# Attention of the last two tiles ended by token halves, the halves' steps alternated, output units placed behind step 7

## What is computed

```python
Q = elu(x @ Wq.T + bq) + 1;  K = elu(x @ Wk.T + bk) + 1;  V = x @ Wv.T + bv
KV = einsum('bnd,bne->bde', K, V);  Z = einsum('bnd,bd->bn', Q, K.sum(axis=1) + 1e-06)
x = layernorm(x + (einsum('bnd,bde->bne', Q, KV) / Z[..., None]) @ Wo.T + bo)      # (8, 512, 128)
# the same rows seen as 8 steps of a gated recurrence for 512 tokens, c: (512, 128)
ft = sigmoid(xt @ wf.T + c @ uf.T + bf);  it = sigmoid(xt @ wi.T + c @ ui.T + bi)
gt = tanh(xt @ wc.T + c @ uc.T + bc);     c = ft * c + it * gt
h = tanh(x @ wo.T + c_final @ uo.T + bo);  x = layernorm(x + h)
```

## Time and profile before

| | before |
|---|---|
| median of the runs | 103.84 us (103.84 to 103.92, 3 runs) |
| profiled execution | 104.32 us |
| its span | 102.4 us |
| granted TensorE clock over the span | 0.983 |

### The profile page before, as it was taken

The page is one execution under the profiler, slowest core; times in us unless marked ns, Lnnn a source line. Parts: engine busy times, 40 slices in busy tenths (PEclk is TensorE's granted clock), DMA queues, the critical chain, the costliest instruction groups (busy, mean ns, idle before and its releaser), DMA issues.

```text
span 102.4 us, 1942 instructions
## 1 busy us (share of the span) xinstructions
PE 93.8 (92%) x615; PEld 80.7 (79%) x615; DVE 80.6 (79%) x235; ACT 67.5 (66%) x140; POOL 42.7 (42%) x65
## 2 busy tenths in 40 slices
PE   5998999999799999999999999999999999979610
PEld 4878788688388978878899899989899999768400
DVE  3226388989999997799589989996544999999870
ACT  1427579479387784966769445599365949779450
POOL 2006198417647238108405803360400056456870
PEclk9999999999999999999999999999999999999985
DMA  2867999000000000000000000000000000145336
GB/s 36 299 250 287 389 400 341 16 0 3 0 0 0 0 0 0 3 6 0 0 0 0 0 0 6 0 3 3 6 0 0 0 0 6 62 143 174 134 102 205
DMA packets 5414, 7.36 MB, mean 72 GB/s; under 512 B 508, under 2 KB 3229, under 8 KB 5405
## 3 DMA queue, kind: packets, MB, share of 16 engines
q1 hardware_dynamic: 4972, 6.92, 19.1%
q10 hardware_dynamic: 432, 0.33, 1.1%
HBM read 5.15 MB, written 2.10 MB: 71 GB/s over the span
## 4 chain that ended last, share of the span: by engine, by line
PE 57%; DVE 27%; issue 5%; ACT 4%; POOL 3%; DVEq 0%; POOLq 0%; ACTq 0%
PE ps_k L408 7%; PE ps_ctx L431 6%; PE ps_q L422 6%; PE ps_ctx L451 5%; DVE stats L1119 5%; PE ps_f L395 4%; DVE x L1108 4%; DVE x L939 3%; PE ps_x L465 2%; DVE s L990 2%; DVE x L954 2%; DVE new L983 2%; POOL rstd L331 2%; PE ps_ctx L441 2%; DVE x L1135 2%
## 5 line engine op out<-in xcount | busy, mean ns | idle before, releaser
L344 POOL TENSOR_TENSOR s_lo<-s,s_hi 128x512 fp32r<-128x512 f32 (+1 forms) x8 | 8.0, 1011 | 24.6 <-ACT s_hi L753 24.6
L331 POOL TENSOR_TENSOR rstd<-var_eps,minus_half 128x4 f32<-128x4 f32 (+1 forms) x9 | 9.2, 1022 | 12.9 <-DVE var_eps L1127 12.8
L315 POOL TENSOR_TENSOR rstd<-var_eps,minus_half 128x4 f32<-128x4 f32 x8 | 8.6, 1078 | 6.6 <-DVE var_eps L930 6.5
L306 POOL TENSOR_TENSOR k_pair<-k_rows 128x256 f32<-128x256 f32 x8 | 6.3, 782 | 9.8 <-DVE k_rows L965 9.8
L939 DVE TENSOR_SCALAR x<-x,stats,rstd 128x128 f32<-128x128 f32 x26 | 10.0, 441 | 0.0
L408 PE MATMUL ps_k<-wkq,x_cols 128*128 128x128 f32 x64 | 9.4, 294 | 0.0
L723 ACT ACTIVATE k_exp<-ps_k,minus_one 128x512 f32<-128x512 f32 x8 | 5.5, 686 | 5.5 <-PE ps_k L416 4.6
L408 PEld LDWEIGHTS ps_k<-wkq,x_cols 128*128 128x128 f32 x64 | 8.7, 209 | 0.3
L790 ACT ACTIVATE x_hi<-ps_x 128x512 fp32r<-128x512 f32 x8 | 4.8, 594 | 6.2 <-PE ps_x L465 6.2
L737 ACT ACTIVATE th_f<-ps_f,half_b 128x256 f32<-128x256 f32 (+1 forms) x11 | 5.8, 530 | 4.4 <-PE ps_f L511 4.2
L422 PE MATMUL ps_q<-x_cols,wkq 128*128 128x512 f32 x16 | 8.2, 597 | 0.0
(11 more groups left out here) (197 smaller groups left out, 291.5 us busy)
## 6 DMA issues: line engine op xcount, KB each, us to landing
x_cols<-xt SPq DMA_DIRECT2D x8, 256.0 KB, 7.3
x_rows<-x SPq DMA_DIRECT2D x8, 256.0 KB, 7.3
out<-x SPq DMA_DIRECT2D x7, 256.0 KB, 2.2
wgate<-w_gate SPq DMA_DIRECT2D x1, 384.0 KB, 6.4
out<-x SPq DMA_DIRECT2D x2, 128.0 KB, 2.0
wkq<-w_kq ACTq DMA_DIRECT2D x1, 131.0 KB, 3.4
wvo_in<-w_vo_in ACTq DMA_DIRECT2D x1, 128.0 KB, 3.3
wout<-w_out SPq DMA_DIRECT2D x1, 128.0 KB, 6.9
```

Of the source, the lines that this page charges most:

```text
L315: nc.gpsimd.tensor_tensor(rstd[:, b], var_eps[:, b], minus_half[:], ALU.pow).then_inc(rstd_ok, 1)
L331: nc.gpsimd.tensor_tensor(part_of(rstd, u, T), part_of(var_eps, u, T), minus_half[:, 0:nt * H].rearrange("p (t c) -> p t c", c=H), ALU.pow ...
L344: nc.gpsimd.tensor_tensor(s_lo[:, t % 2, part], state(t)[:, part], s_hi[:, t % 2, part].bitcast(F32), ALU.subtract).then_inc(slo_ok[k], 1)
```

## The change

The attention of tiles 6 and 7 no longer ends by whole tiles. HALVES lists four halves j: (6, first), (7, first), (6, second), (7, second). Each has its own statistics, variance, root, normalisation, turn, high copy and low part. Halves 0 and 1 are normalised by VectorE, 2 and 3 by ScalarE. They are turned into ps_x1, ps_ctx, ps_x1 and ps_q. The low part of the second halves of tiles 5, 6 and 7 is made by GpSimd from x1_cols instead of by VectorE from PSUM; the first halves' stays on VectorE.

Steps 8 and 9 change places: 8 is now (5, second), 9 is (7, first), so the first and the second half alternate from step 6 on. s_lo of step 8 comes from GpSimd, and that of step 10 is still VectorE's, but now ahead of second_residual(1).

On TensorE out_x(0) and out_x(1), which stood behind gates_s(6) and gates_s(7), now stand behind gates_s(9) and gates_s(10), and gates_x(10) ahead of out_s(0). On ScalarE state_high(10) stands ahead of out_tanh(1), normalise(0) ahead of out_tanh(2), and out_tanh(8) ahead of normalise(5). On VectorE second_normalise(0) stands ahead of second_residual(2). The number of DMAs and their order are unchanged.

```diff
 STEPS = [(0, 0, C), (1, 0, C), (2, 0, C), (3, 0, C), (4, 0, H), (5, 0, H), (4, H, C), (6, 0, H),
-         (7, 0, H), (5, H, C), (6, H, C), (7, H, C)]
+         (5, H, C), (7, 0, H), (6, H, C), (7, H, C)]
...
-SHARED_LN = (0, 6, 7)
+WHOLE = 6
+HALVES = [(6, 0), (7, 0), (6, H), (7, H)]
+SHARED_LN = (0,)
+ACT_HALVES = (2, 3)
...
+        turn_bank = [ps_x1, ps_ctx[:, 0], ps_x1, ps_q]
+        def half_cols(j):
+            return slice(HALVES[j][1] * D, (HALVES[j][1] + H) * D)
+        def turned_half(j):
+            return turn_bank[j][:, half_cols(j)]
...
+            def half_root(j):
+                b, c0 = HALVES[j]
+                pool.wait_ge(var_half_ok, j + 1)
+                nc.gpsimd.tensor_tensor(rstd[:, b, c0:c0 + H], var_eps[:, b, c0:c0 + H], minus_half[:, 0:H],
+                                        ALU.pow).then_inc(rstd_half_ok, 1)
+            def half_shift(j):
+                b, c0 = HALVES[j]
+                pool.wait_ge(minus_mean_half_ok, ACT_HALVES.index(j) + 1)
+                pool.wait_ge(rstd_half_ok, j + 1)
+                nc.gpsimd.tensor_tensor(shift[:, b, c0:c0 + H], minus_mean[:, b, c0:c0 + H], rstd[:, b, c0:c0 + H],
+                                        ALU.mult).then_inc(shift_half_ok, 1)
+            def x1_low(b):
+                if b < WHOLE:
+                    pool.wait_ge(x1c_ok, b + 1)
+                else:
+                    pool.wait_ge(x1c_half_ok, HALVES.index((b, H)) + 1)
+                nc.gpsimd.tensor_tensor(x1_lo[:, b, H * D:], x1_cols[:, b, H:C].rearrange("p c d -> p (c d)"),
+                                        x1_hi[:, b, H * D:].bitcast(F32), ALU.subtract).then_inc(x1lo_pool_ok, 1)
...
@@ -375,13 +418,19 @@
             reciprocal_root(5)
             key_sums(7)
             state_low(4)
-            reciprocal_root(6)
-            first_shift(6)
+            half_root(0)
+            x1_low(5)
+            half_root(1)
             state_low(5)
-            reciprocal_root(7)
-            first_shift(7)
+            half_root(2)
+            half_shift(2)
+            state_low(6)
+            half_root(3)
+            half_shift(3)
             state_low(7)
-            state_low(6)
+            x1_low(6)
+            state_low(8)
+            x1_low(7)
             for u in range(len(UNITS)):
                 second_root(u)
...
+            def x1_half_turned(j):
+                b, c0 = HALVES[j]
+                if j == 0:
+                    pe.wait_ge(x1c_ok, WHOLE)
+                if j == 1:
+                    pe.wait_ge(y_ok, T - 1)
+                if j == 2:
+                    pe.wait_ge(x1c_half_ok, 1)
+                if j == 3:
+                    pe.wait_ge(y_small_ok, T)
+                for i in range(H):
+                    if j in ACT_HALVES:
+                        pe.wait_ge(x1_half_act_ok, ACT_HALVES.index(j) * H + i + 1)
+                    else:
+                        pe.wait_ge(x1_half_ok, j * H + i + 1)
+                    mm = nc.tensor.transpose(turned_half(j)[:, i * D:(i + 1) * D], x1[:, b, c0 + i], ident[:])
+                mm.then_inc(x1t_half_mm, 1)
             gates = [(ps_f, f_ok, f_mm), (ps_i, i_ok, i_mm), (ps_c, c_ok, c_mm)]
...
-                pe.wait_ge(x1hi_ok, t + 1)
+                if t < WHOLE:
+                    pe.wait_ge(x1hi_ok, t + 1)
+                else:
+                    pe.wait_ge(x1hi_half_ok, HALVES.index(STEPS[k][:2]) + 1)
                 nc.tensor.matmul(ps[:, part], wgate_hi[:, g], x1_hi[:, t, part], start=True, stop=False,
...
-                pe.wait_ge(x1lo_ok, t + 1)
+                if t >= WHOLE - 1 and STEPS[k][1] == H:
+                    pe.wait_ge(x1lo_pool_ok, t - WHOLE + 2)
+                elif t >= WHOLE:
+                    pe.wait_ge(x1lo_half_ok, t - WHOLE + 1)
+                else:
+                    pe.wait_ge(x1lo_ok, t + 1)
                 mm = nc.tensor.matmul(ps[:, part], wgate_hi[:, g], x1_lo[:, t, part], start=False, stop=(t == 0),
                                       skip_group_check=True)
...
@@ -676,26 +751,28 @@
             context(7)
             gates_x(5)
             gates_s(5)
+            x1_half_turned(0)
             gates_x(6)
             gates_s(6)
-            x1_turned(6)
-            out_x(0)
+            x1_half_turned(1)
             gates_x(7)
             gates_s(7)
-            x1_turned(7)
-            out_x(1)
             gates_x(8)
             gates_s(8)
+            x1_half_turned(2)
             gates_x(9)
             gates_s(9)
+            out_x(0)
+            gates_x(10)
             out_s(0)
             out_g(0)
-            gates_x(10)
+            x1_half_turned(3)
             gates_s(10)
+            out_x(1)
             add_g(1)
+            gates_x(11)
             out_x(2)
             add_g(2)
-            gates_x(11)
             gates_s(11)
             out_x(3)
...
+            def half_normalise(j):
+                b, c0 = HALVES[j]
+                act.wait_ge(shift_half_ok, ACT_HALVES.index(j) + 1)
+                for c in range(c0, c0 + H):
+                    nc.scalar.activation(x1[:, b, c], x1[:, b, c], ACT.Identity, bias=shift[:, b, c:c + 1],
+                                         scale=rstd[:, b, c:c + 1]).then_inc(x1_half_act_ok, 1)
+            def x1_half_high(j):
+                act.wait_ge(x1t_half_mm, j + 1)
+                nc.scalar.activation(x1_hi[:, HALVES[j][0], half_cols(j)], turned_half(j),
+                                     ACT.Copy).then_inc(x1hi_half_ok, 1)
+            def x1_half_whole(j):
+                b, c0 = HALVES[j]
+                if c0 == 0:
+                    act.wait_ge(x1lo_half_ok, j + 1)
+                nc.scalar.activation(x1_cols[:, b, c0:c0 + H].rearrange("p c d -> p (c d)"), turned_half(j),
+                                     ACT.Copy).then_inc(x1c_half_ok, 1)
...
@@ -844,38 +942,45 @@
             state_high(4)
             x1_whole(5)
             gates_tanh(5)
-            first_normalise(6)
+            x1_half_high(0)
             state_high(5)
-            x1_high(6)
             gates_tanh(6)
-            x1_whole(6)
-            first_normalise(7)
+            x1_half_high(1)
+            x1_half_whole(0)
+            state_high(6)
             gates_tanh(7)
-            x1_high(7)
+            half_normalise(2)
             state_high(7)
-            state_high(6)
+            x1_half_whole(1)
             gates_tanh(8)
-            x1_whole(7)
+            x1_half_high(2)
+            x1_half_whole(2)
+            half_normalise(3)
+            state_high(8)
             gates_tanh(9)
-            state_high(9)
             out_tanh(0)
             g_high(0)
+            x1_half_high(3)
+            x1_half_whole(3)
             gates_tanh(10)
+            state_high(10)
             out_tanh(1)
-            state_high(10)
+            normalise(0)
             out_tanh(2)
             gates_tanh(11)
-            normalise(0)
             out_tanh(3)
             normalise(1)
             out_tanh(4)
             g_high(1)
             normalise(2)
-            for u in range(5, len(UNITS)):
-                out_tanh(u)
-                normalise(u - 2)
-            normalise(len(UNITS) - 2)
-            normalise(len(UNITS) - 1)
+            out_tanh(5)
+            normalise(3)
+            out_tanh(6)
+            normalise(4)
+            out_tanh(7)
+            out_tanh(8)
+            normalise(5)
+            normalise(6)
...
                 ins.then_inc(done, 1)
             def x1_low(b):
+                n = H * D if b == WHOLE - 1 else N
                 dve.wait_ge(x1hi_ok, b + 1)
-                nc.vector.tensor_tensor(x1_lo[:, b], ps_x1[:], x1_hi[:, b].bitcast(F32),
+                nc.vector.tensor_tensor(x1_lo[:, b, 0:n], ps_x1[:, 0:n], x1_hi[:, b, 0:n].bitcast(F32),
                                         ALU.subtract).then_inc(x1lo_ok, 1)
+            def half_low(j):
+                dve.wait_ge(x1hi_half_ok, j + 1)
+                nc.vector.tensor_tensor(x1_lo[:, HALVES[j][0], half_cols(j)], turned_half(j),
+                                        x1_hi[:, HALVES[j][0], half_cols(j)].bitcast(F32),
+                                        ALU.subtract).then_inc(x1lo_half_ok, 1)
+            def half_statistics(j):
+                b, c0 = HALVES[j]
+                dve.wait_ge(y_small_ok if c0 else y_ok, b + 1)
+                nc.vector.bn_stats(stats[:, b, c0:c0 + H].rearrange("p c m -> p (c m)"),
+                                   x1[:, b, c0:c0 + H].rearrange("p c d -> p d c")).then_inc(st_half_ok, 1)
+                dve.wait_ge(st_half_ok, j + 1)
+                nc.vector.tensor_scalar(var_eps[:, b, c0:c0 + H], stats[:, b, c0:c0 + H, 2], 1.0 / D, LN_EPS, ALU.mult,
+                                        ALU.add).then_inc(var_half_ok, 1)
+                if j in ACT_HALVES:
+                    nc.vector.tensor_scalar(minus_mean[:, b, c0:c0 + H], stats[:, b, c0:c0 + H, 1], -1.0, None,
```

(65 more changed lines are left out.)

## The result

The changed kernel took 104.95 us in the median of its four runs (104.4 to 105.4), the kernel before 103.84 (now four runs, 103.45 to 103.92): the ratio is 1.0106, with a 95% interval of 1.0059 to 1.0153. It is slower, by 1.1 us where 0.66 was forecast.

The account below looks back on a forecast made before the run. No engine is full in the rewritten stretch; from second_residual(0) VectorE's own work sets the end until the last unit. Span 102.40 + 0.86 - 0.03 - 0.15 = 103.08; +0.68 on the 103.84 median gives 104.5 us, range 103.7 to 105.0.

Parts of the forecast that it names:

- rival C: Step 8: s(8) waits for GpSimd's x1_low(6), ends 0.7 us later, out_s(0) 0.4 later; 104.9 us in all; chance 0.13.
- tie at half_normalise(1): Attention end: second block at 66.72, GpSimd's state_low(5) at 66.73; GpSimd wins, next VectorE start 0.49 us later.
- rival A: VectorE wins at half_normalise(1), other holds stay; s(6) to out_tanh(0) 0.47 us earlier; 104.05 us; chance 0.18.
- The first variance: Attention end: variance at 62.26 meets GpSimd's s_lo; next start 62.55 instead of 62.34, 0.21 us lost.
- hold at half_statistics(3): Behind s(6): its variance is held until GpSimd's state_low(6) ends at 71.15, covered because new(7) waits for tanh until 71.45.
- the other tie, at s(8): Step 8: s(8) at 74.92, GpSimd's x1_low(6) at 74.97; s(8) taken as not held; this forecast's chance 0.44.
- G: Gain at out_tanh(0), the end of the recurrence stretch: 79.33 against 79.36 us before, about 0.03 us earlier.
- term of 0.86: Unit 1: loss from s(10) to second_residual(3), mostly a new wait for s_hi and tanh costing 0.85 us.
- two idle times that I named as a sign: Unit 1: VectorE idle 0.5 to 0.6 us before s_lo of step 10 and again before second_residual(1).
- The tail: Last unit: out_tanh(8) earlier, but GpSimd's own queue limits the last root's gain to 0.10 to 0.15 us; 0.15 taken.
- B: Half steps: no hold decides, losses of 0.21 and 0.49 us go; not slower, 103.75 us; chance 0.13.
- D: Whole kernel: bound by VectorE's throughput, so the 1.15 us taken from it count; faster, 102.55 us; chance 0.12.

Follow-up runs that it names:

- second set of runs: The changed kernel itself, unaltered, run again beside the first three edits: median 105.06 us, ratio to the kernel before 1.0112.

## Why the prediction was right, and where it was short

- **The reading.** That gains at the half steps would be lost, and that the order at unit 1 would then cost about 0.85 us, is what happened. The forecast was slower by 0.66, the result is 1.1. That the time lies in the range is in part luck: 104.95 stands 0.05 below its upper end, 105.0, the second set of runs gave 105.06, and the range reached so far only to take in rival C.
- **Prices.** The distances between starts carried over. From s(4), s(6), the tanh of step 7 and the start of s(8) came within 0.1 us of the forecast, up to some forty VectorE instructions on.
- **GpSimd's holds.** The tie at half_normalise(1) went to GpSimd and cost 0.49, as forecast; rival A is out, and the run with the pair moved ahead shows that the hold passes through. The first variance cost 0.14 and not 0.21 (next start 0.22 behind it instead of 0.08). I had the next start wait for GpSimd's end; it came at 61.98, 0.06 ahead of it, and in the trace of the kernel before, too, the instruction behind the held variance begins at 67.94, 0.07 ahead of the end of s_lo. The hold at half_statistics(3) was covered by the wait for tanh, as forecast, to within 0.1.
- **The step that failed** is the other tie, at s(8). I had s(8) begin 0.05 us ahead of GpSimd's x1_low(6) (74.92 and 74.97) and gave it to VectorE. In the trace GpSimd began at 74.35 and s(8) at 74.36. From s(4) these are 14.25 and 14.26, where I had 14.38 and 14.33: the start of x1_low(6), which waits for x1_half_whole(2), was 0.13 too late in my sum, and that of s(8) only 0.07. So G came out as -0.41 instead of 0.03. That is rival C, put at 104.9, and the run without this subtraction took the 0.48 back at out_tanh(0). The term that was short is the distance from the third tanh of a step to its s. For step 7 I took about 1.1, but for step 8 1.03 (73.89 to 74.92). The timeline of the kernel before has 1.09 for step 7, its third tanh being that of the earlier trace rows, and 1.10 for the next step:

```profile
72.08 0.42 DVE L990 SCALAR_TENSOR_TENSOR s<-keep,new 128x256 f32<-128x256 f32 x1
...
74.98 0.47 ACT L737 ACTIVATE th_c<-ps_c,wkq 128x256 f32<-128x256 f32 x1
...
76.08 0.43 DVE L990 SCALAR_TENSOR_TENSOR s<-keep,new 128x256 f32<-128x256 f32 x1
```

In the trace of after it is 1.11 (73.25 to 74.36), and x1_low(6) stands 1.10 behind the same tanh, where I had 1.08. With 1.10 for both distances the sum has them start together. A lead of 0.05 at the end of a chain of sums was no ground for 0.44 against 0.13; the two should have stood about even. Nor does a small lead protect: the block held at 66.15 had one of 0.03, that of the earlier trace rows one of 0.07.
- **A page against the trace.** The traces of after show s(8) and keep(9), both with two inputs in SBUF, held beside a GpSimd subtraction (1.01 and 0.69 us for 0.42). By the Trainium skill, SBUF — State Buffer, section "Who interferes with whom", such an instruction contends with a GpSimd instruction that reads SBUF. The trace agrees for GpSimd's subtractions. Beside its roots, which read SBUF as well, it shows no hold of VectorE: new(5) lay inside one and kept its 0.42 us, while the root took 0.80 instead of 0.70.

```profile
64.53 0.80 POOL L352 TENSOR_TENSOR rstd<-var_eps,minus_half 128x2 f32<-128x2 f32 x1 [0.96 <-DVE var_eps L1082]
64.70 0.42 DVE L1115 SCALAR_TENSOR_TENSOR new<-th_i,th_c 128x256 f32<-128x256 f32 x1
```

- **Unit 1.** Forecast 2.13 from s(10) to statistics(1), 2.12 measured, and 6.45 from s(10) to second_residual(3) against 5.60: the term of 0.86 is 0.85. The run of the kernel before with this order alone confirms it (0.90). In the changed kernel undoing it gives back only 0.46, for the reason told below. Of the two idle times that I named as a sign, the first is there (0.48), the second nearly gone (0.06). No gain from the early low part shows.
- **The tail.** Forecast 0.15, the trace gives 0.13, and 0.10 in the kernel before.
- **Rivals B and D** fall: the holds are real, and giving VectorE back 0.34 us of work made the kernel faster.
- **What I had missed.** TensorE's moved out_x(0) and out_x(1) don't show in the sum of the changed kernel. Once the wait at unit 1 is gone, TensorE's queue takes back 0.24 us, and with gates_x(11) moved behind unit 2 that is won. That it is just these two that fill the queue there is read from the order, not tried by itself.

With these terms set right the sum is 0.41 + 0.85 - 0.13 = 1.13 us, against 1.12 in the traces and 1.11 in the medians.

## What to carry to other kernels

Work that is moved from a VectorE with idle time to GpSimd isn't free: where one of VectorE's normalisations, variances or instructions with two inputs in SBUF meets a GpSimd subtraction, it stands still until that ends (0.49 and 0.59 us were lost here beside subtractions of 0.73), and it can be the one on the path. Before a hand-written order is changed in a stage where an engine runs without a gap, look for every instruction that waits for another engine's answer to the one just done, and keep one piece of independent work between the two. A tie of less than 0.1 us in a worked-out schedule decides nothing; give both sides an equal chance, and take the tie away if you may.

## What the runs showed of the hardware that I had not expected

An instruction of VectorE that starts a hundredth of a microsecond behind a GpSimd subtraction is held: s(8), 128x256, took 1.01 us instead of 0.42 in four profiled executions alike, and 0.43 with the subtraction gone. A start 0.03 us ahead did not help either (the block at 66.15). The held instruction ended by about the same time behind GpSimd's in each case of its kind: s(8) and keep(9), with two inputs in SBUF, 0.28 us, the normalisation 0.08, the variances 0.02 to 0.03. So one whose own end would lie as late anyway loses nothing: keep(8) began at 73.03, inside a subtraction that ended at 73.17, and kept its 0.42. Statistics, and residuals that read PSUM, kept their time beside the same subtractions (statistics 0.42 at 69.57 beside that of 69.84, a pair of residuals 0.60 at 62.77 beside that of 62.83 to 63.57). The order of such ties repeats: counted from one early instruction, two executions of the changed kernel agree within 0.02 us over 40 us, while their starts differ by 0.3 us (s(4) at 60.10 and 59.80).
